# A delta-rule block: the state summed in PSUM, two tiles' joins interleaved, the experts' weights folded later, roots and pieces of the second inversion in another order

## The chip, the cores and the metric

One core of one Trainium2 chip. The time is microseconds (us) of device time for one launch, as the median of several runs; the profile is of one execution, recorded by the hardware profiler.

## The reference, cut to what matters

```python
# x: 4 sequences, 1024 tokens, 128 channels, float32
def delta(x, gates_w, gates_b, lr_w, lr_b, out_w, out_b):
    q, k, v = split(x @ gates_w + gates_b, 3)
    lr = x @ lr_w + lr_b
    k = k / norm(k)
    A = tril(k @ k.T, -1) + eye(T)          # T = 1024
    u = solve_triangular(A, v, lower=True)
    y = (q @ k.T) @ (lr * u)
    return y @ out_w + out_b
xn = layernorm(x)
h  = xn + delta(layernorm(xn), ...)
x1 = x + h + mlp(layernorm(h))              # 128 -> 128 -> 128, relu
z  = layernorm(x1)
chosen = argmax(z @ gate_w.T)               # 8 experts
out = x1 + z + z @ expert_w[chosen].T
```

The score matrix has no mask, so y = q @ M with M the sum over all tokens of k (lr u) as an outer product. The solve is done by tiles of 128 tokens with a running state S, the sum of k u over the tiles so far: u_t = T_t (v_t |k| - k_t S), where T_t is the inverse of the tile's lower triangle.

## The kernel before, in words

Everything is float32. T = 8 tiles of 128 tokens, each with NS = 4 sequences, so each tile is 128 x 512. Every engine has its program written out by hand in its own block (`@block.tensor`, `@block.vector`, `@block.scalar`, `@block.gpsimd`, `@block.sync`), in the order in which it is to run; semaphores are the only link. Nothing is planned or scheduled by a tool, so what a line waits for also holds up what stands behind it on its engine.

**Start (0 to 39 us).** VectorE takes the layernorm statistics (`stats`, `scales`, lines 688 to 714), ScalarE the square roots (`root`, L358), and the normalised tiles (`xh`) are written in pieces of one sequence by GpSimd, ScalarE and VectorE, as the tables XH_POOL, XH_ACT and XH_DVE say. TensorE turns a tile (`xT_`, L1048), multiplies by the weights of k (`kT_`, L1065), and takes the Gram matrix of the tile (`gram`, L1053); ScalarE evacuates each (`xnT_` L368, `kT_` L372, `gg_` L387). `k_` (L1048, evacuated by L376) turns k back for tiles 0 to 3 in the loop's second half. The sync engine copies the diagonal 32 x 32 blocks of the Gram matrices by DMA into `gd` (L264, 4 DMAs a tile).

**Inversions.** The 32 x 32 diagonal blocks of tiles 0 to 3 (group 0) are inverted together on VectorE, then those of tiles 4 to 7 (group 1): `prepare` (transpose L759, reciprocal L763, product L765), 31 steps of `eliminate` (L782 and L789), `plain_` and `place` (transposes L797 and L806, copies L811), `rest` (L816, L817). The steps of group 1 are cut into pieces between which VectorE does its share of the fold.

**Joins.** From the inverted 32-blocks TensorE builds the 128 x 128 inverse `tt_all` of each tile, with small matmuls and an evacuation after each: `ya` (L1124), `za` (L1133, L1136, L1141), `y64_` (L1150), `t12` (L1160). ScalarE's functions of the same names evacuate them; for tiles of group 1 VectorE takes `yb`, `zb` and `t12`. ScalarE's `diagonals` (L445, L448) and VectorE's `place` bring the inverted blocks to where the joins read them; PLACES says for which tiles at a time.

**Fold.** For each tile t, in the order of the loop at L1243: `ks` (k S, L1214), the rest of tile t's join, the next tile's `ya`, `w_` (u, L1220), `m_` of the tile before (L1232, summed in PSUM over all tiles), the next tile's `za`, `s_` (k u of this tile, L1224), and the next tile's `y64_`. VectorE's `rv_` (L839) makes the right side from the product ks. The state is in SBUF (`sm`): after each tile VectorE adds the four products that TensorE left in PSUM to it, one addition a sequence (`s_`, L844), and the next `ks` of a sequence waits for its addition; for tile 0 ScalarE copies them (L533).

**Experts' weights.** They are centred by matmuls of 512 columns (`expert_` L1110, `expert_one` L1114), two halves, placed between the joins and the folds of tiles 0 and 1; ScalarE evacuates them (L436).

**Tail (122 to 232 us).** M is multiplied out, and then for each tile: y (`delta`), second layernorm, MLP, choice of expert, 8 experts' products (L1324) and the pick of the chosen one on VectorE (L969).

```python
for t in range(T):            # TensorE, start
    kT_(t)
    if t + 1 < T: xT_(t + 1)
    gram(t)
    if t >= TG: k_(t - TG)
```

## Time and profile before

| | |
|---|---|
| median of the runs | 236.33 us (3 runs, 234.13 to 236.86) |
| the profiled execution | 233.88 us |
| its span, first to last instruction | 232.1 us |
| TensorE busy | 203.6 us (88%) |
| VectorE busy | 164.5 us (71%) |
| ScalarE busy | 122.8 us (53%) |
| GpSimd busy | 58.9 us (25%) |
| mean granted TensorE clock | 0.924 of full |

Some 1.8 us of the execution's time lie outside its span. The profile gives TensorE's granted clock per stretch: 1.00 is 2.4 GHz, 0.50 is 1.2 GHz, and values between are a mean of the two.

### The profile page before, as it was taken

To read this page: it belongs to the slowest core of one execution; us is meant where nothing else is said; L and a number is where in the kernel's file an instruction comes from. 1 tells how busy PE (TensorE), PEld (TensorE's weight loads), DVE (VectorE), ACT (ScalarE), POOL (GpSimd) and SP (SyncE) were. 2 spreads that over 40 slices of the span, in tenths; PEclk is the share of its full clock that TensorE was granted. 3 is DMA by queue.
4 is the path that set the end of the run, shared out by engine and by line. 5 is a ranking of instruction groups with operands and counts; after the bars stand their busy time and mean duration, and the time that the engine had idled before them with its cause. 6 is when DMAs were issued, how large, how long until landed. Compare 5 with 4: busy or idle time off the path is not lost.

```text
span 232.1 us, 4284 instructions
## 1 busy us (share of the span) xinstructions
PE 203.6 (88%) x1347; PEld 146.6 (63%) x1347; DVE 164.5 (71%) x748; ACT 122.8 (53%) x324; POOL 58.9 (25%) x73
## 2 busy tenths in 40 slices
PE   0795988999999759999989498999999999999980
PEld 0454666977799658989987285565656565565520
DVE  7994999999489854142353825969696878787785
ACT  2585565789585652434672555354646373735130
POOL 7255800000000069740200402206060606022020
PEclk9999799999999975557999859999999999999998
DMA  5951011000000000000000000001010101010111
GB/s 137 265 138 26 3 24 21 6 3 0 3 4 0 3 0 0 4 0 0 4 0 3 1 0 0 0 3 47 0 45 1 48 1 45 0 45 3 45 47 45
DMA packets 15612, 5.92 MB, mean 26 GB/s; under 512 B 5468, under 2 KB 15590, under 8 KB 15590
## 3 DMA queue, kind: packets, MB, share of 16 engines
q1 hardware_dynamic: 15014, 5.58, 9.6%
q8 instruction: 11, 0.18, 0.3%
q10 hardware_dynamic: 576, 0.07, 0.2%
q14 instruction: 11, 0.09, 0.1%
HBM read 3.09 MB, written 2.10 MB: 22 GB/s over the span
## 4 chain that ended last, share of the span: by engine, by line
PE 72%; DVE 8%; ACT 5%; issue 3%; DVEq 0%; ACTq 0%
PE ps L1324 22%; PE ps L1053 8%; PE ps L1048 5%; PE ps L1220 4%; PE ps L1224 4%; PE ps L1214 4%; PE ps L1232 3%; PE ps L1080 3%; PE ps L1299 3%; PE ps L1315 3%; PE ps L1150 2%; PE ps L1160 2%; DVE kT_all L969 2%; PE ps L1124 2%; ACT tt_all L448 1%
## 5 line engine op out<-in xcount | busy, mean ns | idle before, releaser
L1324 PE MATMUL ps<-ewC,kT_all 128*128 128x512 f32 x128 | 60.4, 596 | 0.9 <-DVE kT_all L969 0.8
L969 DVE COPY_PREDICATED kT_all<-mask,ps 128x256 f32<-128x256 int32 x112 | 48.9, 436 | 17.2 <-ACT kT_all L634 11.1
L1324 PEld LDWEIGHTS ps<-ewC,kT_all 128*128 128x128 f32 x128 | 22.0, 190 | 19.2 <-issue 19.2
L315 POOL TENSOR_SCALAR h_all<-x_all,mv,rr 128x128 f32<-128x128 f32 x16 | 12.4, 790 | 54.9 <-DVE da_all L817 54.9
L333 POOL TENSOR_TENSOR x_all<-x_all,kT_all 128x512 f32<-128x512 f32 x7 | 8.9, 1270 | 55.4 <-ACT kT_all L640 55.4
L789 DVE TENSOR_TENSOR xi<-xi,prod 128x60 f32<-128x60 f32 (+13 forms) x116 | 19.5, 207 | 0.3
L782 DVE TENSOR_TENSOR prod<-lts,xi 128x60 f32<-128x60 f32 (+13 forms) x116 | 19.3, 206 | 0.3
L328 POOL TENSOR_TENSOR x_all<-x_all,h_all 128x512 f32<-128x512 f32 (+1 forms) x9 | 10.3, 1147 | 30.9 <-DVE h_all L900 24.1
L611 ACT ACTIVATE k_all<-h_all,nb,rr 128x128 f32<-128x128 f32 x32 | 14.0, 484 | 4.2 <-DVE nb L921 4.2
L839 DVE SCALAR_TENSOR_TENSOR rv<-v_all,nk,ps 128x128 f32<-128x128 f32 x28 | 8.4, 345 | 10.0 <-PE ps L1214 9.5
L1048 PE MATMUL ps<-ident,h_all 128*128 128x128 f32 x32 | 6.0, 320 | 9.4 <-ACT h_all L363 7.0
L634 ACT COPY kT_all<-ps 128x256 f32<-128x256 f32 x16 | 5.8, 363 | 15.6 <-PE ps L1324 15.6
L1048 PEld LDWEIGHTS ps<-ident,h_all 128*128 128x128 f32 x32 | 4.7, 168 | 14.9 <-issue 14.6
L299 POOL TENSOR_SCALAR h_all<-x_all,mv,rr 128x128 f32<-128x128 f32 x14 | 11.1, 804 | 10.6 <-DVE rr L710 10.6
L322 POOL TENSOR_TENSOR x_all<-x_all,b2s 128x512 f32<-128x512 f32 x8 | 10.1, 1268 | 12.0 <-ACT h_all L527 12.0
L1220 PE MATMUL ps<-rv,tt_all 128*128 128x128 f32 x64 | 10.9, 323 | 1.4 <-DVE tt_all L832 0.6
L1053 PE MATMUL ps<-kT_all 128*128 128x128 f32 x64 | 9.9, 303 | 2.3 <-ACT kT_all L372 2.3
L1053 PEld LDWEIGHTS ps<-w2s,k_all 128*128 128x128 f32 x64 | 9.2, 208 | 4.0 <-issue 3.3
L1053 PEld LDWEIGHTS ps<-kT_all 128*128 128x128 f32 x64 | 8.4, 205 | 4.5 <-ACT kT_all L372 4.4
L1053 PEld LDWEIGHTS ps<-gg_all,xnT_all 128*128 128x128 f32 x64 | 9.1, 209 | 3.0 <-issue 2.4
L1220 PEld LDWEIGHTS ps<-rv,tt_all 128*128 128x128 f32 x64 | 9.4, 225 | 2.1 <-DVE rv L839 1.4
L1315 PEld LDWEIGHTS ps<-gwC,kT_all 128*128 128x128 f32 x64 | 8.5, 193 | 3.3 <-issue 3.3
(160 smaller groups left out, 437.4 us busy)
## 6 DMA issues: line engine op xcount, KB each, us to landing
x_all<-in_L_attn_x_dram SPq DMA_DIRECT2D x7, 256.0 KB, 5.5
out_dram<-x_all SPq DMA_DIRECT2D x7, 256.0 KB, 2.3
ew<-in_L_ffn_expert_w_dram SPq DMA_DIRECT2D x1, 512.0 KB
gd<-gg_all SPq DMA_DIRECT2D x28, 16.0 KB, 1.8
x_all<-in_L_attn_x_dram SPq DMA_DIRECT2D x2, 128.0 KB, 2.6
out_dram<-x_all SPq DMA_DIRECT2D x2, 128.0 KB, 1.8
wall<-in_L_attn_gates_w_dram SPq DMA_DIRECT2D x2, 64.0 KB
wall<-in_L_attn_gates_w_dram ACTq DMA_DIRECT2D x1, 64.0 KB, 2.6
```

What stands on the lines that cost most here:

```text
L299: nc.gpsimd.tensor_scalar(xh[:, t, n], x_all[:, t, n], mv[:, 0, t, n, 0:1], rr[:, t, 1, n:n + 1], ALU.subtract, ALU.mult).then_inc(xh_pool, 1)
L315: last = nc.gpsimd.tensor_scalar(h_all[:, t, n], x_all[:, t, n], mv[:, 0, t, n, 0:1], rr[:, t, 0, n:n + 1], ALU.subtract, ALU.mult)
L328: nc.gpsimd.tensor_tensor(x_all[:, t, span(of)], x_all[:, t, span(of)], h_all[:, t, span(of)], ALU.add).then_inc(xb_ready, len(of))
L611: nc.scalar.activation(tn[t % 2][:, n], h_all[:, t, n], ACT.Identity, bias=nb2[:, t, n:n + 1], scale=rr2[:, 0, t, n:n + 1]).then_inc(tn_re ...
L782: nc.vector.tensor_tensor(mul[half], lts[:, j, lo:hi].unsqueeze(2).broadcast_to([P, hi - lo, w]), xi[g][:, j, 0:w].unsqueeze(1).broadcast_ ...
L789: nc.vector.tensor_tensor(xi[g][:, lo:hi, 0:w], xi[g][:, lo:hi, 0:w], mul[half], ALU.subtract).then_inc(elim, 1)
L969: nc.vector.copy_predicated(sel[t % 2][:, n], mask[t % 2][:, n, E - 1 - e].unsqueeze(2).broadcast_to([P, 2, F]), ps[:, b:b + 2, (e % EH) * ...
L1048: last = nc.tensor.transpose(tiles(bank)[:, n], src(n), ident[:])
L1053: last = nc.tensor.matmul(tiles(bank)[:, n], lhsT(n), rhs(n), start=True, stop=True)
L1220: nc.tensor.matmul(ps[:, n, C:2 * C], tt_all[:, t, n], rv[:, n], start=True, stop=True).then_inc(w_mm, 1)
L1315: last = nc.tensor.matmul(ps[:, 3, n * E:n * E + E], x1T[t % 2][:, n], gwC[:], start=True, stop=True)
L1324: last = nc.tensor.matmul(ps[:, 4 + 2 * half + n, :], x1T[t % 2][:, 2 * pair + n], ewC[:, EH * half:EH * half + EH, :].rearrange("p e f -> ...
```

## The change

It has five parts.

1. **State in PSUM.** `s_` on TensorE no longer writes a product per tile that VectorE adds: it sums into bank 6 over all tiles (start on the first matmul of tile 0, no stop before tile 6), and signals once, after the fourth sequence. ScalarE copies the whole bank to `sm` (one 128 x 512 copy a tile); `ks` waits for that copy. VectorE's 24 additions (tiles 1 to 6) and ScalarE's 4 copies of tile 0 go. `yb` and `zb` move from bank 6 to bank 7.
2. **Joins.** `ya(1)` and `za(1)` stand before the first fold, `y64_(1)` ahead of the first `ks`, and on ScalarE rv0 is made early (so `norms`, the transpose of the norms, stands inside the first elimination). In the fold at t = 3, `ya(4)` stands between the two halves of `m_(2)`.
3. **Experts' weights.** `expert_` and `expert_one` move behind the fold, among the first `delta`s and transposes of the tail; the weights' halves use banks 4 and 5.
4. **Start.** `root(4)` and `root(5)` stand earlier on ScalarE, VectorE's statistics of tiles 6 and 7 stand behind the scaling of tiles 4 and 5, `xh` of tiles 4 to 7 has three pieces on GpSimd and one on VectorE (2 and 2 before), and `k_` stands ahead of `gram` (TensorE) and of `gg_` (ScalarE).
5. **Second inversion.** The pieces are cut at steps 9 and 22 (9, 19 and 27 before), both transposes stand ahead of `rv` of tile 3, the copies are made for tile 4 first and for tiles 5 to 7 behind; the product at L765 leaves out what the elimination does not read. The residual's `h_` of sequences 2 and 3 moves from ScalarE to VectorE.

```diff
-    XH_POOL = [()] + [LOW] * (T - 1)
+    XH_POOL = [()] + [LOW] * (TG - 1) + [(0, 1, 2)] * TG
-    XH_DVE = [HIGH] + [(3,)] * (TG - 1) + [HIGH] * TG
+    XH_DVE = [HIGH] + [(3,)] * (T - 1)
...
-        PLACES = ((0, 0, AHEAD), (0, AHEAD, TG), (1, 0, TG))
+        PLACES = ((0, 0, AHEAD), (0, AHEAD, TG), (1, 0, AHEAD), (1, AHEAD, TG))
...
@@ ScalarE, the start @@
             for t in range(T):
+                if t == TG - 2:
+                    root(4)
                 kT_(t)
+                if t == TG - 1:
+                    root(5)
                 if t + 1 < T:
                     xnT_(t + 1)
...
-                gg_(t)
-                if t == TG - 2:
-                    root(4)
                 if t >= TG:
                     k_(t - TG)
+                gg_(t)
+                if t == TG:
+                    nkl_(0)
...
@@ ScalarE, the fold @@
-            def s_(n):
-                act.wait_ge(s_mm, n + 1)
-                nc.scalar.copy(sm[:, n], ps[:, n, 2 * C:3 * C]).then_inc(s_ready, 1)
+            def s_(t):
+                act.wait_ge(s_mm, t + 1)
+                nc.scalar.copy(rows(sm[:, :, :]), ps[:, 6, :]).then_inc(s_ready, 1)
...
@@ VectorE, the start @@
+            stats(3)
             for j in range(2, len(PARTS)):
-                if j % 2 == 0:
-                    if j > 2:
-                        stats(j)
-                    stats(j + 1)
+                if j > 3:
+                    stats(j)
                 scales(j)
...
@@ VectorE, the product of prepare @@
-                nc.vector.tensor_tensor(lts[:], lt[:], rd[:].unsqueeze(1).broadcast_to([P, Q, Q]), ALU.mult).then_inc(elim, 1)
+                for lo, hi in ((0, 12), (12, Q - 1)):
+                    nc.vector.tensor_tensor(lts[:, lo:hi, lo + 1:Q], lt[:, lo:hi, lo + 1:Q],
...
@@ VectorE, the order @@
-            eliminate(1, 9, 19)
-            s_all(1)
+            eliminate(1, 9, 22)
             rv_all(2)
-            eliminate(1, 19, 27)
-            s_all(2)
+            eliminate(1, 22, Q - 1)
+            plain_(1)
+            turned(1)
             rv_all(3)
-            eliminate(1, 27, Q - 1)
-            plain_(1)
             place(2)
...
@@ TensorE @@
             def ks(t, n):
-                pe.wait_ge(s_ready, (t - 1) * NS + n + 1)
+                pe.wait_ge(s_ready, t)
...
             def s_(t, n):
                 pe.wait_ge(w_ready, t * NS + n + 1)
-                nc.tensor.matmul(ps[:, n, 2 * C:3 * C], k_all[:, t, n], ww[t % 2][:, n, 0:C], start=True,
-                                 stop=True).then_inc(s_mm, 1)
+                last = nc.tensor.matmul(tiles(6)[:, n], k_all[:, t, n], ww[t % 2][:, n, 0:C], start=t == 0 and n == 0,
+                                        stop=t == T - 2, skip_group_check=True)
+                if n == NS - 1:
+                    last.then_inc(s_mm, 1)
...
             delta(0, HIGH, 3)
+            expert_(0)
             delta(1)
+            expert_one(0)
             tT_(0, LOW)
+            expert_(1)
             hid_(0, LOW)
             tT_(0, HIGH, 6)
+            expert_one(1)
             out_(0, LOW)
```

On VectorE, the end of the second inversion. `xi` and `prod` are the elimination, `rv` the right side of the fold, `sm` the state; before, the last steps stand behind tile 2's addition and tile 3's right side:

```order
L844 TENSOR_TENSOR sm<-ps,sm 128x128 x4
L839 SCALAR_TENSOR_TENSOR rv<-v_all,nk,ps 128x128 x4
L782 TENSOR_TENSOR prod<-lts,xi 128x28 x2
L789 TENSOR_TENSOR xi<-xi,prod 128x2x14 x2
...
L789 TENSOR_TENSOR xi<-xi,prod 128x16
L797 STREAM_TRANSPOSE d_all<-xi 128x512
L806 STREAM_TRANSPOSE dT_all<-d_all 128x512
L811 COPY tt_all<-dT_all 32x16x32 x2
```

The same place of the changed kernel:

```order
L785 TENSOR_TENSOR xi<-xi,prod 128x16
L793 STREAM_TRANSPOSE d_all<-xi 128x512
L798 STREAM_TRANSPOSE dT_all<-d_all 128x512
L839 SCALAR_TENSOR_TENSOR rv<-v_all,nk,ps 128x128 x4
L808 COPY tt_all<-dT_all 32x4x32 x2
L817 COPY da_all<-d_all 32x16x32
L821 COPY yT<-ps 32x128
```

The right side of tile 3 now stands behind all of the elimination and both transposes, and no addition of the state is left.

On TensorE, from the first fold (L1220, then L1222) to the second tile's `ks` (L1214, then L1216). Before:

```order
L1220 MATMUL ps<-rv,tt_all 128x128 x4
L1224 MATMUL ps<-ww,k_all 128x128 x4
L1133 MATMUL ps<-yT,da_all 32x32 x4
L1136 MATMUL ps<-da_all,yT 32x32 x4
L1141 MATMUL ps<-yT,d_all 32x32 x4
L1110 MATMUL ps<-ewT,cent 128x512
L1214 MATMUL ps<-sm,kT_all 128x128 x4
```

Changed:

```order
L1136 MATMUL ps<-yT,da_all 32x32 x4
L1139 MATMUL ps<-da_all,yT 32x32 x4
L1144 MATMUL ps<-yT,d_all 32x32 x4
L1222 MATMUL ps<-rv,tt_all 128x128 x4
L1226 MATMUL ps<-ww,k_all 128x128 x4
L1153 MATMUL ps<-tt_all,gg_all 64x64 x4
L1216 MATMUL ps<-sm,kT_all 128x128 x4
```

`za(1)` went ahead of the first fold, the experts' matmul away, and `y64_(1)` in its place.

## Rows read from the trace of the kernel before

**Rows 1.** The page, second part: granted clock in 40 slices of 5.8 us.

```profile
PEclk9999799999999975557999859999999999999998
```

**Rows 2.** Windows: length; busy PE, PEld, DVE, ACT, POOL; granted clock; DMA share, GB/s.

```profile
18.70:22.50 3.80, 1.68 (x10) 0.88 (x9) 1.66 (x7) 1.39 (x3) 2.49 (x4) 1.00 0.17 26
...
78.40:84.00 5.60, 2.60 (x32) 2.29 (x32) 4.87 (x13) 4.47 (x12) 0.57 (x1) 1.00 0.01 3
84.00:107.80 23.80, 23.65 (x184) 21.61 (x186) 7.10 (x22) 8.05 (x27) 15.56 (x19) 0.50 0.00 1
...
126.00:131.70 5.70, 3.10 (x20) 2.15 (x18) 4.94 (x17) 1.97 (x6) 2.71 (x3) 1.00 0.01 1
131.70:138.60 6.90, 5.90 (x23) 4.83 (x23) 2.18 (x12) 4.22 (x11) 0.00 (x0) 0.51 0.00 0
```

**Rows 3.** Chain that ended last, fold: start us, us, what.

```profile
57.01 1.13 PE ps L1220 x8
...
61.00 0.89 PE ps L1214 x8
...
88.31 2.00 PE ps L1214 x8
...
99.98 2.00 PE ps L1214 x8
...
110.24 1.09 PE ps L1214 x8
...
117.12 1.09 PE ps L1214 x8
...
122.33 1.06 PE ps L1277 x4
```

**Rows 4.** Timeline of the start, all engines: start us, us, instruction, [idle before].

```profile
19.66 0.25 DVE L710 RECIPROCAL rr<-sd 128x16 f32<-128x16 f32 x1 [0.99 <-ACT sd L358]
...
20.01 3.16 POOL L299 TENSOR_SCALAR h_all<-x_all,mv,rr 128x128 f32<-128x128 f32 x4 [4.31 <-DVE rr L710]
...
25.65 1.97 DVE L759 STREAM_TRANSPOSE lt<-gd 128x1024 f32<-128x1024 f32 x1
```

**Rows 5.** Sync's last DMA of tiles 0 to 2, and its landing.

```profile
22.01 0.60 SPq L264 DMA_DIRECT2D gd<-gg_all  x1
...
DMA to landing us min/median/max: 1.8/1.8/2.9
```

**Rows 6.** The chain in the start's loop, one tile.

```profile
30.04 1.16 PE ps L1053 x8
31.20 0.44 PE ps L1048 x4
...
32.54 0.70 ACT kT_all L372
```

**Rows 7.** Timeline of VectorE: end of the first inversion, parts of the second.

```profile
45.14 1.07 DVE L797 STREAM_TRANSPOSE d_all<-xi 128x512 f32<-128x512 f32 x1
...
51.80 1.23 DVE L765 TENSOR_TENSOR lts<-lt,rd 128x1024 f32<-128x1024 f32 x1
...
69.75 1.12 DVE L839 SCALAR_TENSOR_TENSOR rv<-v_all,nk,ps 128x128 f32<-128x128 f32 x4 [0.73 <-PE ps L1214]
...
79.39 1.06 DVE L797 STREAM_TRANSPOSE d_all<-xi 128x512 f32<-128x512 f32 x1
```

**Rows 8.** Timeline, ScalarE before the first fold and the experts' copy.

```profile
50.29 0.41 ACT L445 COPY da_all<-d_all 32x128 f32<-32x128 f32 x1
...
59.23 0.59 ACT L436 COPY ewC<-ps 128x512 f32<-128x512 f32 x1
```

**Rows 9.** Timeline of TensorE at the start of the tail.

```profile
129.87 0.44 PE L1048 MATMUL ps<-ident,k_all 128*128 128x128 f32 x2 [1.78 <-ACT k_all L611]
131.12 0.67 PE L1299 MATMUL ps<-k_all,w1s 128*128 128x256 f32 x2 [0.81 <-ACT k_all L617]
132.59 0.69 PE L1048 MATMUL ps<-ident,k_all 128*128 128x128 f32 x2 [0.80 <-ACT k_all L611]
```

More of the change, by code:

```diff
@@ L197, in parts @@
             return [(half, lo, hi) for half, lo, hi in ((0, j + 1, j + 1 + top), (1, j + 1 + top, Q)) if hi > lo]
-        ELIM = 3 + sum(2 * len(parts(j)) for j in range(Q - 1))
+        ELIM = 4 + sum(2 * len(parts(j)) for j in range(Q - 1))
         AHEAD = 1
+        PREP_BANK = (4, 4, 4, 4, 4, 5)
         block = ctx.enter_context(nc.Block())
@@ L494, in _ @@
             k_(4)
+            for n in range(NS):
+                rv0(n)
             v_(2)
@@ L510, in _ @@
             za(0)
+            v_(6)
+            y64_(0)
             v_(7)
-            y64_(0)
-            for n in range(NS):
-                rv0(n)
+            ya(1)
+            yb(1)
             t12(0)
+            zb(1)
+            za(1)
             def w_(t, n):
@@ L568, in _ @@
                 if t == TG - 1:
-                    for n in range(NS):
-                        lrw(t, n)
                     diagonals(2)
                     ya(t + 1)
-                    za(t + 1)
-                else:
-                    za(t + 1)
-                    for n in range(NS):
-                        lrw(t, n)
+                za(t + 1)
+                s_(t)
                 y64_(t + 1)
-                for i in range(max(0, 2 * (t - TG) + 1), 2 * (t - TG) + 3):
-                    h_(i)
-            h_(T - 1)
+                for n in range(NS):
+                    lrw(t, n)
+                if t == TG - 1:
+                    diagonals(3)
             t = T - 1
@@ L773, in eliminate @@
             def eliminate(g, start, stop):
-                done = ELIM * g + 3 + sum(2 * len(parts(j)) for j in range(start))
+                done = ELIM * g + 4 + sum(2 * len(parts(j)) for j in range(start))
                 sub_at = [done, done]
@@ L848, in rv_all @@
                     rv_(t, n)
-            def s_all(t):
-                for n in range(NS):
-                    s_(t, n)
             prepare(0)
-            eliminate(0, 0, Q - 1)
+            eliminate(0, 0, 14)
+            norms(0)
+            eliminate(0, 14, Q - 1)
             plain_(0)
+            turned(0)
             place(0)
@@ L865, in _ @@
             rv_all(1)
-            eliminate(1, 9, 19)
-            s_all(1)
+            eliminate(1, 9, 22)
             rv_all(2)
-            eliminate(1, 19, 27)
-            s_all(2)
+            eliminate(1, 22, Q - 1)
+            plain_(1)
+            turned(1)
             rv_all(3)
-            eliminate(1, 27, Q - 1)
-            plain_(1)
             place(2)
             rest(1)
+            yb(TG)
+            norms(1)
+            zb(TG)
+            place(3)
             dve.wait_ge(nk_done, NG)
-            for t in range(TG - 1, T):
-                if t >= TG:
-                    rv_all(t)
-                    t12(t)
+            dve.wait_ge(xT_mm, T)
+            for t in range(TG, T):
+                rv_all(t)
+                t12(t)
                 if t + 1 < T:
@@ L1120, in ya @@
                 joined(pe, zb_ready, t)
-                for bank, lo, ready in ((5, 0, ya_mm), (6, 2 * Q, yb_mm)):
+                for bank, lo, ready in ((5, 0, ya_mm), (7, 2 * Q, yb_mm)):
                     hi = lo + Q
@@ L1241, in _ @@
                 s_(0, n)
-            za(1)
-            expert_(1)
+            y64_(1)
             for t in range(1, T):
@@ L1258, in _ @@
                 if t == 1:
-                    pe.wait_ge(prep_ready, 6)
-                for n in range(NS):
+                    pe.wait_ge(prep_ready, 4)
+                for n in LOW:
                     m_(t - 1, n)
@@ L1263, in _ @@
                     ya(t + 1)
+                for n in HIGH:
+                    m_(t - 1, n)
                 if joins:
```

99 lines of the change are left out of this document (44 added, 55 removed).

## The prediction

> **What bounds the kernel now.** I read the page first, for the clock, then the windows of its odd slices, then the chain that ended last, then the timelines of the engines that the chain names. The execution took 233.88 us for a span of 232.1, so 1.8 us lie outside; the median of the runs is 2.45 us above it. A difference of 2% (4.7 us) is about what a measurement of this kernel tells from none.
>
> The slices show TensorE's clock at the full 2.4 GHz except in three places: one in the start, a long one at 84 to 108 us, one early in the tail [rows 1]. In the windows, each low stretch follows one in which TensorE waited much: busy 1.68 of 3.80 us before the first (0.50, that is 1.2 GHz), 2.60 of 5.60 before the long one, 3.10 of 5.70 before the third [rows 2]. The long one is the dearest thing in this profile: TensorE is busy 23.65 of 23.80 us there, at 0.50. The chain shows what it costs: from one `ks` to the next it is 99.98 - 88.31 = 11.67 us at the low level and 117.12 - 110.24 = 6.88 us at the full one [rows 3], so 4.8 us a tile. The fold from 57 us on is bound by TensorE's own matmuls, except at one place: after the right side of tile 3, VectorE still has the end of the second inversion before it; its first transpose starts only at 79.39 [rows 7], and the joins of tile 4 wait for it: 3.0 of the 5.60 us from 78.4 to 84.0 are idle on TensorE. That wait costs twice, as idle time and as low clock behind it.
>
> **The start.** Tile 4's pieces wait for the root, which stands behind an evacuation: VectorE was idle 0.99 us for it, GpSimd 4.31 us, and its four pieces take 3.16 us, 0.79 each [rows 4]. Now the root is due when its input is there, some 2.7 us earlier (about 17.2 in place of 20.01 for GpSimd's start). GpSimd has three pieces a tile for four tiles: 3 x 0.79 = 2.4 us a tile, tile 4 ready at 19.6, tile 7 at 26.8. TensorE, idle for 2.1 us in the window at 18.7 to 22.5 [rows 2], gets its input at once. The root of tiles 6 and 7 is then bound by their statistics, so VectorE ends its pieces at 22.0, and the copies for the inversion at 22.5. In TensorE's loop a tile takes 1.16 + 0.44 + 0.87 + 0.70 and some gaps = 3.24 us along the chain [rows 6]; the 0.44 of `k_` moves under the 0.70 of ScalarE's copy, so 2.80. Bounds for the first part: nothing, to 3.8 us (the 2.1 idle and half of the 3.4 us at low clock). I take 3.0, since VectorE's order holds the copy of tile 3; with four times 0.44 the first `v_` comes 3.0 + 1.8 = 4.8 us earlier. GpSimd's 2.4 us a tile is inside 2.8, so it is just hidden; were its pieces 20% dearer, it would bound the loop.
>
> VectorE does not gain as much, because of a queue that the change leaves alone: the sync engine issues the 12 DMAs of tiles 0 to 2 one behind the other, the last at 22.01, landing 1.8 us later [rows 5], so the first inversion can start at 23.9 at the soonest, where it started at 25.65 [rows 4]. That is 1.75 us, not 3.1. The cut product (372 + 361 elements of 1024, by 1.23 us [rows 7]: 0.9 us in two) gives 0.3 us to each inversion, and the norms' transpose takes 0.2 of the first. An inversion took 45.14 - 25.65 = 19.5 us [rows 4, 7], so the blocks, with two transposes of 1.07, come at 45.5, 1.9 us earlier than now, and the second inversion starts some 2 us behind, at 47.5.
>
> **Up to the first fold.** ScalarE starts `diagonals` at 50.29 [rows 8]; it will do so at 45.5 (both the blocks and the copy of `v_(5)` are there then). Between there and the first `w_` (57.01 [rows 3]) ScalarE is the bound, and it keeps its work: rv0 leaves (1.2 us), `v_(6)` comes in (0.5). `w_` starts at 52.2, 4.8 us earlier. From there to `ks` of tile 1 it took 61.00 - 57.01 = 4.0 us [rows 3], with `za(1)` and the experts' 1.10 us in it; now w 1.1, s 0.9, then one copy of 0.6 (a 128 x 512 copy took 0.59 [rows 8]) beside `y64_(1)`, 2.7 us. `ks` of tile 1 at 54.95: 6.05 us earlier.
>
> **The fold.** VectorE loses the six times four additions, of about a microsecond a tile. A `ks` waited in its sequence for one addition; now all wait for a copy of 0.6 us after the last product, and `y64_` of 0.6 us stands in the gap. Bounds: 0 if hidden, 0.6 a tile if it is not (3.6 in all); I take 0.05 a tile. ScalarE has the copy, but `h_` went to VectorE, four pieces of 0.3 us in stages in which VectorE has 2 us of work: hidden.
>
> The second inversion has 19.2 us of its own work from 47.5 on, and two right sides of 1.12 us [rows 7] between: nothing else now, so it ends at 69.0, and the two transposes of 1.06 at 71.2. (The 31 steps are 15.4 of the 19.2, half a microsecond each: cut 9 is at 55.6, when tile 1's right side is due, cut 22 at 63.7, when tile 2's is.) TensorE asks for tile 3's right side at 70.3, so the wait is put here now: 1.2 us of idle in place of the 3.0. Then `w_` of tile 3 at 71.5 (78.4 before), the copies for tile 4 alone behind 1.12 us of right side [rows 7], and half of `m_(2)` under them. To `ks` of tile 4 it is 5.2 us at full clock (the same products as from `w_` to `ks` in a tile of 6.88 us): 76.7, where it was 88.31 [rows 3]. 11.6 us earlier.
>
> From there to the end of the fold the work is the same. Before: 117.12 - 88.31 = 28.8 us for three tiles, two of them at the low clock; now 3 x 6.93 = 20.8: 8.0 us more. Sum so far 19.6 us. From `ks` of tile 7 to the end of `m_`, 5.2 us [rows 3], nothing changes.
>
> **The clock.** Everything above hangs on it. The window of the long low stretch shows that the clock does not come back by TensorE's being busy (23.65 of 23.80 us [rows 2]), so a fall inside the fold is dear: 23.8 us at 4.8 us a tile of 11.67 is 9.8 us. The idle time of the changed kernel is 1.2 us before the inverted blocks (VectorE's and ScalarE's gain differ), about 1 us before `y64_(0)` and 1.2 us before `w_` of tile 3, each among small matmuls; so none as long as the 2.1 and 3.0 us in rows 2; but the experts' matmuls, which filled the joins, are gone.
>
> Here the Trainium skill says otherwise: in TensorE: Matmul & The Clock Gate, section "What's actually happening", "the default state is throttled, and activity releases the throttle". By that rule a fall in the fold would end soon and cost 1 or 2 us. The trace disagrees, with the 23.65 busy us at 0.50.
>
> **The tail.** TensorE was idle 1.78 + 0.81 + 0.80 us there, and then ran 6.90 us at 0.51 [rows 9, 2]. The experts' four matmuls (about 1.1 us each: 4.3 us) fill these gaps, and overflow them by 0.9. ScalarE's two copies of 0.59 [rows 8] delay the first transposes by 0.3 to 0.8. If the clock stays up, the 5.90 busy us at 0.51 become some 3: a gain of 2.1 net; if it falls all the same, a loss of 1.5. I take a gain of 1.5, since the gap before the low stretch is what is filled.
>
> **Sum.** 6.05 to `ks` of tile 1, 5.55 more to `ks` of tile 4, 8.0 in the tiles behind, 1.5 in the tail: 21.1 us. 233.88 - 21.1 = 212.8. The runs' median stood 2.45 above this execution; half of it, for low stretches that a run has more of, gives 214.0.
>
> **Rivals.**
> - *The clock falls in the fold* for a stretch like the one of before, now after the joins of tile 0 or before `w_` of tile 3. For it: three shorter waits stand where the clock held before, and nothing fills them. Against it: 1.2 us of idle is the most in one piece, and less than before each of the three falls. 214 + 9.8 = 223.8. With a quick release it is 216.
> - *The copy of the state and the new order are not hidden*: `ks` waits 0.6 us on six tiles, GpSimd's 12 pieces bound the start (1 us): 214 + 4.6 = 218.6. That the sum in PSUM saves nothing is this case too: the 24 additions lay beside TensorE's work but for the waits.
> - *Slower.* The clock falls at the joins of tile 0, where the experts' matmuls are gone, and does not come back before the tail, as it did not for 23.8 us of this fold's work [rows 2]. Then the seven tiles cost 4.8 us more each than in my sum: 214 + 33 = 247. It is slower than before from the fifth tile at low clock on. Against it: the same fold ran at full clock until 84.0 and again from 107.8 on [rows 1, 2].
>
> **How the numbers follow.** Forecast 0.58, a fall in the fold 0.25, the copy not hidden 0.12, the slow clock throughout 0.05. The first three are all faster by over 4.7 us. Faster 0.93, within 2% 0.03, slower 0.04. The time is the first case's, 214.0. Down, the start's and tail's bounds give 5 us (209); up, the range takes in the fall at 223.8: 209 to 225.
>
> **What would show it.** The inversion's first transpose at 24, the first `w_` near 52, `ks` of tile 4 near 77, no window at 0.50 between 70 and 100, the tile-to-tile step 6.9 throughout; 24 additions less on VectorE; an idle of about 1.2 us before tile 3's `w_`, put down to VectorE. I am wrong if the long low stretch is there again, elsewhere; if `ks` waits on ScalarE's copy by over 0.3 us a tile; or if the first inversion is not held by the DMAs.

## The result and the profile after

The changed kernel took 214.20 us (median of 4 runs, 213.98 to 214.80), the kernel before, on the same chip, 236.19 us (median of 4, 234.13 to 236.86): a ratio of 0.909, 95% interval 0.903 to 0.915. The profiled execution took 213.98 us for a span of 212.2. Span against span that is 19.9 us less, where the forecast's sum had 21.1. In 34 later executions the kernel before ran at one of two levels, 228.5 to 230.6 us with a mean granted clock of 0.949 to 0.959 (the lower) or 233.7 to 237.2 us with 0.923 to 0.925 (the upper), and the runs compared here lie at the upper one.

Two lines of the page, which answer to [rows 1]:

```profile
span 212.2 us, 4273 instructions
...
PEclk9999999999999999999999999999999999999998
```

The three places below 9 in [rows 1] are gone; the last slice is the end of the program. Windows of after, which answer to [rows 2]: the end of the second inversion, the four tiles behind it, and two stretches of the early tail. Columns: the stretch, its length, then busy time and instructions of PE, PEld, DVE, ACT and POOL, then the granted clock, the DMA share and GB/s.

```profile
69.00:75.00 6.00, 5.37 (x60) 4.72 (x59) 5.29 (x17) 4.78 (x16) 0.68 (x1) 1.00 0.00 0
75.00:99.00 24.00, 23.47 (x308) 20.98 (x306) 11.18 (x37) 14.14 (x47) 17.08 (x20) 1.00 0.01 3
112.00:118.00 6.00, 5.01 (x24) 2.75 (x23) 3.25 (x14) 4.68 (x12) 1.26 (x1) 1.00 0.00 0
118.00:124.00 6.00, 5.37 (x33) 3.83 (x32) 3.22 (x16) 3.08 (x9) 1.27 (x1) 1.00 0.00 0
```

TensorE is busy 5.37 of 6.00 us where it had 2.60 of 5.60, and 5.01 of 6.00 at the head of the tail where it had 3.10 of 5.70; behind each, the clock is 1.00 where it was 0.50 and 0.51. The chain that ended last, after, answers to [rows 3] (start, length, engine, tile and line; `L1216` is `ks`, `L1222` is `w_`, `L1279` the start of what follows the fold):

```profile
22.27 1.82 DMA gd<-gg_all
24.12 2.00 DVE lt L751
...
46.76 0.56 PE ps L1127 x16
...
53.08 0.88 PE ps L1222 x6
...
56.13 0.50 PE ps L1216 x2
...
72.41 1.24 PE ps L1222 x8
...
77.25 0.59 ACT sm L535
77.89 1.16 PE ps L1216 x8
...
84.91 1.16 PE ps L1216 x8
...
91.93 1.16 PE ps L1216 x8
...
98.95 1.16 PE ps L1216 x8
...
104.23 1.06 PE ps L1279 x4
```

Against before: `ks` of tile 1 comes 4.9 us earlier (61.00 to 56.13), `ks` of tile 4 10.4 us (88.31 to 77.89), `ks` of tile 7 18.2 us (117.12 to 98.95), and the rest, from 104.23 to the end of the span, is 108.0 us where it was 109.8. The step from `ks` to `ks` is 7.02 us from tile 4 to 5, 5 to 6 and 6 to 7, where it was 11.67, 10.26 and 6.88.

### The profile page after: what moved, and what is told of

It is laid out like the page before. It is cut to its first block, busy times and chain, and to the rows that moved or that the text cites. A ratio compares the mean times of both kernels' runs of the same rounds, so it can differ in the third digit from the quotient of the medians.

```text
span 212.2 us, 4273 instructions
## 1 busy us (share of the span) xinstructions
PE 190.4 (90%) x1347; PEld 135.0 (64%) x1347; DVE 161.2 (76%) x740; ACT 119.0 (56%) x314; POOL 62.4 (29%) x77
## 4 chain that ended last, share of the span: by engine, by line
PE 58%; DVE 24%; SPq 9%; issue 4%; ACT 3%; DMA 1%; DVEq 0%; ACTq 0%
PE ps L1326 24%; DVE xi L785 6%; DVE prod L778 6%; PE ps L1057 6%; PE ps L1052 4%; SPq L267 3%; PE ps L1222 3%; PE ps L1317 3%; PE ps L1301 3%; PE ps L1226 3%; PE ps L1236 3%; SPq L249 3%; PE ps L1216 2%; DVE kT_all L973 2%; SPq L259 2%
## 5 line engine op out<-in xcount | busy, mean ns | idle before, releaser
L318 POOL TENSOR_SCALAR h_all<-x_all,mv,rr 128x128 f32<-128x128 f32 x16 | 12.8, 816 | 45.5 <-DVE da_all L817 45.5
L302 POOL TENSOR_SCALAR h_all<-x_all,mv,rr 128x128 f32<-128x128 f32 x18 | 14.2, 806 | 7.6 <-DVE rr L703 7.6
L1057 PEld LDWEIGHTS ps<-w2s,k_all 128*128 128x128 f32 x64 | 8.5, 191 | 4.1 <-issue 3.8
L839 DVE SCALAR_TENSOR_TENSOR rv<-v_all,nk,ps 128x128 f32<-128x128 f32 x28 | 7.8, 338 | 4.3 <-PE ps L1216 4.3
L1222 PE MATMUL ps<-rv,tt_all 128*128 128x128 f32 x64 | 9.2, 286 | 1.5 <-DVE tt_all L832 0.6
L1057 PEld LDWEIGHTS ps<-gg_all,xnT_all 128*128 128x128 f32 x64 | 8.3, 191 | 3.3 <-issue 2.6
L608 ACT ACTIVATE k_all<-ps,cols 128x512 f32<-128x512 f32 (+1 forms) x9 | 6.6, 731 | 5.9 <-PE ps L1052 5.9
```

The costliest lines, as they stand in the source:

```text
L302: nc.gpsimd.tensor_scalar(xh[:, t, n], x_all[:, t, n], mv[:, 0, t, n, 0:1], rr[:, t, 1, n:n + 1], ALU.subtract, ALU.mult).then_inc(xh_pool, 1)
L318: last = nc.gpsimd.tensor_scalar(h_all[:, t, n], x_all[:, t, n], mv[:, 0, t, n, 0:1], rr[:, t, 0, n:n + 1], ALU.subtract, ALU.mult)
L1057: last = nc.tensor.matmul(tiles(bank)[:, n], lhsT(n), rhs(n), start=True, stop=True)
L1222: nc.tensor.matmul(ps[:, n, C:2 * C], tt_all[:, t, n], rv[:, n], start=True, stop=True).then_inc(w_mm, 1)
```

## The experiments

The runs stand in four series, each on another chip and each with runs of the kernel before in it: experiments 1 to 3, 4 to 7, 8 to 10, and 11. A kernel is compared with before at one of the two levels and with the changed kernel's 214.2 us; the changed kernel itself ran again in the second series alone (experiment 7). The lower level of before had medians of 228.7, 228.8, 229.1 and 229.0 us in the four, so a difference of under half a microsecond between series says little. For such differences two intervals of the trace are steadier, `ks` of tile 1 to `ks` of tile 4 and `ks` of tile 4 to `ks` of tile 7: in two traces of the changed kernel they are 21.76 and 21.06, and 21.77 and 21.06 us.

**1. Only the long wait filled.** The kernel before, with ten matmuls of 128 columns, whose result is not used, in TensorE's wait for the second inversion.

```diff
                 if t + 1 == TG:
+                    for i in range(7):
+                        nc.tensor.matmul(ps[:, 7, 0:C], ident[:], ident[:], start=True, stop=True)
                     ya(t + 1)
+                    for i in range(3):
+                        nc.tensor.matmul(ps[:, 7, 0:C], ident[:], ident[:], start=True, stop=True)
```

> The kernel before, with ten matmuls of 128 columns added on TensorE (into a corner of PSUM that nobody reads), seven before the joins of tile 4 and three behind their first step: work in place of the wait for the second inversion, nothing else changed. If the clock falls because TensorE waits there, the stretch at 0.50 from 84 to 108 us goes and with it 8 to 10 us: 226 to 228 us against 236. Rival: the low stretch comes from the fold's own work or from the chip, whatever TensorE does in the wait: then it stays, and the time is the same or 0.5 us longer.

Measured: 224.91 us (224.66 to 226.02, 4 runs), the lower level of before in the same series being 228.45 to 228.74 and the upper 236.84 to 237.16; ratio to the lower level 0.985 (0.981 to 0.988). The row of the granted clock, and the window where before had 23.65 busy us at 0.50 [rows 2]:

```profile
PEclk9999699999999999999999589999999999999998
```

```profile
84.00:108.00 24.00, 23.58 (x310) 21.36 (x309) 10.80 (x40) 15.24 (x50) 17.38 (x20) 1.00 0.01 2
```

What is left of TensorE's idle time there, 0.59 and 0.17 us where the kernel before had 2.12 and 1.03:

```profile
83.23 0.59 PE L1124 MATMUL ps<-tt_all,gg_all 32*32 32x32 f32 x16 [0.59 <-DVE tt_all L811]
...
84.85 0.31 PE L1133 MATMUL ps<-yT,da_all 32*32 32x32 f32 x5 [0.17 <-ACT yT L453]
```

Nothing of the kernel's own work was removed, and the kernel's own matmuls came no earlier to these places (83.23 where it was 82.53). So the low stretch comes from TensorE's being idle ahead of it. Filling the wait is worth 3.8 us against the lower level of before and 12 us against the upper, and the time is below the 226 to 228 us expected. The stretches in the start and in the tail stay. This is the claim under the whole forecast, shown with one edit.

**2. How thin is the margin?** The changed kernel, with one or three more transposes of some 1.1 us on VectorE (into a buffer that is no longer read) ahead of tile 3's right side. The edit with one; the other has `range(3)`.

```diff
             turned(1)
+            for i in range(1):
+                dve.wait_ge(dT_done, 2 + i)
+                nc.vector.transpose(xi[0][:].rearrange("p r k -> p (r k)"), xi[1][:].rearrange("p r k -> p k r")).then_inc(dT_done, 1)
             rv_all(3)
```

> As the one with three transposes, with one: TensorE waits 1.6 us. It shows how near the changed kernel stands to a fall. If it has room: 215.3 us and full clock. Rival: the fall is near, and some or all of the runs have a low stretch: 220 to 225 us.

> The changed kernel, with three more transposes of 1.1 us on VectorE (into a buffer that is free by then) ahead of the right side of tile 3, so that TensorE waits about 3.8 us there in place of 0.6. If the wait alone brings the clock down: 3.3 us for the transposes and up to 10 for a stretch at 0.50 behind it, 221 to 228 us against 214. Rival: the clock does not depend on this wait: 217.5 us and no window at 0.50.

Measured: one transpose 219.23 us (215.96, 220.13, 220.02, 218.44), three 221.74 us (220.03, 223.45, 219.10, 223.91). The granted clock goes with the time: 0.998, 0.967, 0.967, 0.972 and 0.982, 0.960, 0.989, 0.961. TensorE's timeline at tile 3's `w_` in the first and the second kernel, the idle time ahead and its releaser in brackets:

```profile
74.33 1.26 PE L1225 MATMUL ps<-rv,tt_all 128*128 128x128 f32 x8 [1.61 <-DVE rv L839]
```

```profile
76.96 1.97 PE L1225 MATMUL ps<-rv,tt_all 128*128 128x128 f32 x8 [3.75 <-DVE rv L839]
```

The profiled runs are the fastest of the four with one transpose (215.96) and the second fastest with three (220.03). The wait grew from 0.56 to 1.61 and 3.75 us. With 1.61 the clock held in the profiled run, and `ks` of tile 1 to `ks` of tile 4 took 22.84 us, 1.08 more than in the changed kernel: the length of the transpose. The rest of that run's 1.8 us lay ahead of the edit, in the start, where the changed kernel's own two traces differ by 0.7 us (experiment 7). In the other three runs the mean clock was 0.967 to 0.972 and the cost 4.2 to 5.9 us; they have no trace, so that their low stretch lies behind this wait is argued, not shown. Behind the wait of 3.75 eight `w_` matmuls took 1.97 us in place of 1.26. The price of a wait here is its length plus, in some runs, a low stretch.

**3. The order of the second inversion undone**, its cuts at 19 and 27 and its end behind tile 3's right side, with VectorE's copies for tiles 4 to 7 together, as before; the rest of the change stays, ScalarE's order, the shorter product and `h_` on VectorE among it.

```diff
-            eliminate(1, 9, 22)
+            eliminate(1, 9, 19)
             rv_all(2)
-            eliminate(1, 22, Q - 1)
+            eliminate(1, 19, 27)
+            rv_all(3)
+            eliminate(1, 27, Q - 1)
             plain_(1)
             turned(1)
-            rv_all(3)
             place(2)
+            place(3)
+            norms(1)
             rest(1)
             yb(TG)
-            norms(1)
             zb(TG)
-            place(3)
```

> The changed kernel with the order of the second inversion as before: cuts at 9, 19 and 27, right side of tile 3 ahead of the last steps and the transposes, and the copies for tiles 4 to 7 in one piece. By my steps the end of the inversion moves from ahead of tile 3's right side to behind it: tile 3's fold comes 2 us earlier, but the joins of tile 4 wait some 3 us for the last steps, the transposes and the copies; structurally 1 to 2 us slower, 216, and 224 to 226 if that wait brings the clock down. Rival: the order of the pieces is worth nothing by itself, since the additions that went have freed VectorE: 214 to 214.5.

Measured: 221.32 us (221.15 to 222.43, 4 runs), 7.1 us above the changed kernel, with clocks of 0.968 to 0.976. That lies between the 216 us expected without a fall of the clock and the 224 to 226 with one. Its timeline of TensorE and its windows (columns as above):

```profile
76.90 0.87 PE L1128 MATMUL ps<-tt_all,gg_all 32*32 32x32 f32 x16 [2.15 <-DVE tt_all L808]
82.97 2.07 PE L1217 MATMUL ps<-sm,kT_all 128*128 128x128 f32 x8
93.23 1.16 PE L1217 MATMUL ps<-sm,kT_all 128*128 128x128 f32 x8
```

```profile
70.90:76.90 6.00, 3.29 (x28) 2.87 (x28) 5.21 (x21) 3.34 (x12) 0.00 (x0) 0.99 0.00 0
76.90:85.50 8.60, 8.60 (x73) 7.68 (x74) 3.42 (x10) 4.21 (x13) 6.94 (x9) 0.50 0.01 2
```

The wait of 2.15 us is that of before, and it brings the low stretch back: `ks` of tile 4 is 5.1 us later than in the changed kernel, and one step is 10.26 us. Of the four pieces that were undone or added alone (experiments 3 to 6), this order is the largest.

**4. The start alone**, on the kernel before: the third piece of tiles 4 to 7 on GpSimd, the roots moved up, `k_` ahead of the Gram copy, and VectorE's statistics in the changed kernel's order (the last two are not shown).

```diff
-    XH_POOL = [()] + [LOW] * (T - 1)
+    XH_POOL = [()] + [LOW] * (TG - 1) + [(0, 1, 2)] * TG
...
-    XH_DVE = [HIGH] + [(3,)] * (TG - 1) + [HIGH] * TG
+    XH_DVE = [HIGH] + [(3,)] * (T - 1)
...
+                if t == TG - 2:
+                    root(4)
                 kT_(t)
+                if t == TG - 1:
+                    root(5)
...
```

> The kernel before with the start part alone (GpSimd's third piece for tiles 4 to 7, the roots of the second group before their turn, k_ ahead of the Gram copy). Theory (the start moves the joins earlier, and the later stages are bound by VectorE's two inversions and by the clock): the first v_ some 4 us earlier than 39.33 and the first inversion's transpose near 24, but ks of tile 1 only some 1.8 us earlier than 61.00, because the diagonals wait for the first inversion; then the second inversion, which keeps its order, is waited for as before (3 us idle before tile 4's ya), and the long stretch at 0.50 stays. Time 1.5 to 3 us below the kernel before at the same level: about 234 against 236.5, or 226.5 against 228.6. Rival (the start is worth its full 4 us down to the end): 224 to 225 against 228.6.

Measured: 225.24 us (224.52 to 225.46, 4 runs), all at clocks of 0.951 to 0.959; before at that level, same series, 228.46 to 228.86. That is 3.6 us below its median of 228.8, about the rival's number (224 to 225). The chain:

```profile
22.29 1.82 DMA gd<-gg_all
24.13 1.99 DVE lt L758
...
46.88 0.56 PE ps L1123 x16
...
57.27 0.89 PE ps L1213 x8
...
84.59 2.00 PE ps L1213 x8
```

`ks` of tile 1 and of tile 4 are both 3.7 us earlier than in [rows 3]. My theory had the first inversion hold the joins; but before, it was done by about 47.3 (45.14 us in [rows 7], plus two transposes of 1.07), and `diagonals` started only at 50.29 [rows 8], behind the `v_` copies. The inversion had 3 us to spare, so the start's gain went through: in this run `diagonals` starts at 46.40, behind a `v_` copy again. The wait for the second inversion stayed at 2.12 us and the low stretch behind it too, as the theory had it, but with one step of `ks` slowed in place of two.

**5. The experts' weights back among the joins** and in the fold's first tiles, with ScalarE's two copies of them.

```diff
             ya(0)
             v_(6)
+            expert_(0)
             za(0)
             v_(7)
             y64_(0)
+            expert_one(0)
             ya(1)
...
-            expert_(0)
             delta(1)
-            expert_one(0)
             tT_(0, LOW)
-            expert_(1)
...
```

> The changed kernel with the experts' four matmuls back among the joins and the fold's first tile, the two copies of ScalarE too. Theory (they fill gaps of the tail, which starves TensorE's clock without them): ks of tile 1 some 1 to 1.5 us later than 56.13 (ScalarE's 1.2 us of copies stand before the w_ copies), the tail from the end of m_ to the end 109.8 us as before in place of 108.0, with the stretch at 0.50 near 128 us back: 216 to 218. Rival (the tail's gaps are ScalarE's anyway and the clock holds): 214.5 to 215.5, PEclk at 9 to the end.

Measured: 218.79 us (217.65 to 219.84, 4 runs), clocks 0.979 to 0.981. Row of the clock, `ks` of tile 1 in the chain, and two rows of TensorE's timeline in the tail:

```profile
PEclk9999999999999999999996799999999999999997
```

```profile
58.39 0.89 PE ps L1219 x8
```

```profile
114.51 0.65 PE L1052 MATMUL ps<-ident,k_all 128*128 128x128 f32 x2 [1.78 <-ACT k_all L604]
115.97 1.19 PE L1307 MATMUL ps<-k_all,w1s 128*128 128x256 f32 x2 [0.81 <-ACT k_all L610]
```

The gaps of 1.78 and 0.81 us in [rows 9] are back, and so is the low stretch, now at about 113 to 124 us. The move is worth 4.6 us on the medians, more than the 2 to 4 expected. In the profiled run, the fastest of the four, it is 2.3 at `ks` of tile 1, which I had priced at 1 to 1.5, another 0.5 by `ks` of tile 4, and 0.9 behind the fold. That run's first inversion also started 0.5 us earlier (23.64), so the joins lost 2.8 us rather than 2.3.

**6. The state added up on VectorE again**, from a product in each tile's own bank, where the changed kernel sums in PSUM.

```diff
+            def sadd(t):
+                for n in range(NS):
+                    dve.wait_ge(s_mm, t * NS + n + 1)
+                    nc.vector.tensor_tensor(sm[:, n], ps[:, n, 2 * C:3 * C], sm[:, n], ALU.add).then_inc(s_ready, 1)
...
-            eliminate(1, 9, 22)
+            eliminate(1, 9, 20)
+            sadd(1)
             rv_all(2)
-            eliminate(1, 22, Q - 1)
+            eliminate(1, 20, 29)
+            sadd(2)
+            eliminate(1, 29, Q - 1)
```

> The changed kernel with the state added up on VectorE out of SBUF again, 24 additions of some 0.26 us, in the new order of the second inversion. Theory (their price is the delay of the second inversion): two groups of four stand before the inversion's end, so tile 3's right side comes 2 us later than 72.0 and ks of tile 4 some 2 us later than 77.9; 216 to 217 if the clock holds, 219 to 224 if the wait of 2.5 us before tile 3's w_ lets it fall, as in the run with three transposes more. Rival (the additions lay beside TensorE's work, as before): 214 to 214.8, ks of tile 4 within 0.5 us of 77.9.

Measured: 216.27 us as a median, but in two pairs: 214.80 and 214.91 us at clocks of 0.996 and 0.997, 217.64 and 218.17 at 0.980 and 0.981. The rows of the profiled run (one of the pair at the higher clock), `ks` of tile 2, tile 3's `w_`, and `ks` of tiles 4 and 5:

```profile
63.88 1.16 PE L1225 MATMUL ps<-sm,kT_all 128*128 128x128 f32 x8 [1.03 <-DVE sm L850]
...
73.83 1.26 PE L1231 MATMUL ps<-rv,tt_all 128*128 128x128 f32 x8 [1.34 <-DVE rv L838]
79.19 1.16 PE L1225 MATMUL ps<-sm,kT_all 128*128 128x128 f32 x8
86.07 1.16 PE L1225 MATMUL ps<-sm,kT_all 128*128 128x128 f32 x8
```

The additions make `ks` of tile 2 wait 1.03 us, since here they stand behind eleven steps of the inversion, and delay tile 3's `w_` by 1.4 us; a part is won back, since a tile then takes 6.88 us again. The span is 213.1, 0.9 above the changed kernel's. So at the full clock the sum in PSUM is worth 0.7 us. In two runs of four the mean clock was lower, and there it is worth 3.7; which of the two waits, 1.03 or 1.34 us, that goes with isn't shown, since these runs have no trace. The cuts differ too (9, 20 and 29), so other places for the additions could cost less.

**7. The changed kernel once more**, unedited.

> The changed kernel itself, once more, on this chip, to see whether it has two levels as the kernel before has (228.6 and 236.9). Theory (its waits are too short for the clock to fall): 213.9 to 214.9 in every run, granted clock 0.99 to 1.0. Rival (the thin margin that the runs with one and three transposes more showed is crossed by itself on some runs): one or more runs of 217 to 221, clock below 0.98.

Measured: 214.19 us (214.81, 213.93, 214.09, 214.29), clocks 0.993 to 1.0. In eight runs it has one level, where the kernel before has two. The profiled run (214.81) is 0.8 us slower than the first profiled one, and nearly all of that is in the start: the first inversion's transpose at 24.76 in place of 24.12, `ks` of tile 1 at 56.83 in place of 56.13, and 21.77 us from there to `ks` of tile 4.

**8. The copy of the state in two halves**, each `ks` waiting for its own.

```diff
-                nc.scalar.copy(rows(sm[:, :, :]), ps[:, 6, :]).then_inc(s_ready, 1)
+                for of in (LOW, HIGH):
+                    nc.scalar.copy(sm[:, span(of)], tiles(6)[:, span(of)]).then_inc(s_ready, 1)
...
-                pe.wait_ge(s_ready, t)
+                pe.wait_ge(s_ready, 2 * t - 1 + n // 2)
```

> The changed kernel with ScalarE's copy of the summed state in two halves, each ks waiting for its half alone. Theory (the one copy of 0.59 us that four ks wait for is the 0.14 us by which a tile takes 7.02 in place of 6.88): the step from ks to ks falls to 6.88 and the span by 0.8 to 1.0 us, to 211.3; time 213.3. Rival (two copies cost ScalarE more than they free, some 0.2 us a tile in fixed cost, and push the y64_ copy and the left sides): step 7.0 to 7.1, time 214.2 to 215.

Measured: 213.19, 213.53 and 213.78 us at clocks of 0.994 to 1.0, and 216.06 at 0.947; median 213.66. The profiled run is the one at 0.947. In its chain, `ks` of the last four tiles:

```profile
77.99 1.10 PE ps L1217 x8
...
84.89 1.09 PE ps L1217 x8
...
91.78 1.09 PE ps L1217 x8
...
98.68 1.09 PE ps L1217 x8
```

A step of 6.90 in place of 7.02: the term that the forecast had at 0.05 a tile was 0.14, and the halves give 0.12 of it back. From `w_` of tile 0 to `ks` of tile 7 the fold takes 45.31 us in place of 45.94; six steps would give 0.7, but tile 3's `w_` now waits 0.78 us for its right side. The three runs at the higher clock, 213.5 in the middle, are 0.7 below the changed kernel's 214.2, which ran in another series; experiment 10 has the step at 6.88 in a run at 0.998.

**9. The cuts of the second inversion moved to where VectorE has no wait**, 10 and 25 in place of 9 and 22.

```diff
-            eliminate(1, 0, 9)
+            eliminate(1, 0, 10)
...
-            eliminate(1, 9, 22)
+            eliminate(1, 10, 25)
             rv_all(2)
-            eliminate(1, 22, Q - 1)
+            eliminate(1, 25, Q - 1)
```

> The changed kernel with the cuts of the second inversion placed where VectorE has no wait: the right side of tile 1 after 10 steps in place of 9, that of tile 2 after 25 in place of 22. Theory (VectorE waits 0.84 and 1.26 us for TensorE before these two right sides, and this wait is what makes tile 3's right side late): the second inversion's transposes come 1.5 to 2 us earlier (69.98 to some 68.2), tile 3's w_ no longer waits for them (0.56 us of TensorE's idle goes), ks of tile 4 at 77.2 to 77.4 in place of 77.89, time 213.5 to 213.8. Rival (what the steps gain, ks of tiles 1 and 2 lose by a right side that now comes late): ks of tile 4 at 77.8 or later, time 214.2 to 215.

Measured: 215.15 us (214.94 to 215.46, 4 runs), 1 us slower than the changed kernel and slightly above the rival's range. From `ks` of tile 1 to `ks` of tile 4 it took 22.46 us in place of 21.76, so 0.7 of it is the cuts' own. I had read the changed kernel's waits in sum and put one of 1.26 us to tile 2's right side. Its timeline shows that this piece had no wait at all (rows of VectorE, changed kernel):

```profile
56.77 1.12 DVE L839 SCALAR_TENSOR_TENSOR rv<-v_all,nk,ps 128x128 f32<-128x128 f32 x4 [0.84 <-PE ps L1216]
64.76 1.11 DVE L839 SCALAR_TENSOR_TENSOR rv<-v_all,nk,ps 128x128 f32<-128x128 f32 x4
```

The 1.26 us stood before tile 4's right side. With the cut at 25 tile 2's came at 66.00, and TensorE waited for it (same kernel, TensorE):

```profile
66.39 1.26 PE L1222 MATMUL ps<-rv,tt_all 128*128 128x128 f32 x8 [0.72 <-DVE rv L839]
73.50 1.13 PE L1222 MATMUL ps<-rv,tt_all 128*128 128x128 f32 x8 [0.56 <-ACT tt_all L483]
```

**10. The edits of 8 and 9 together, and the eight DMAs of the later weights issued behind the Gram matrix's 12** of the first inversion.

```diff
-            for dst, src in ((wo[:, :], out_w), (w1s[:, :], w1), (w2s[:, :], w2), (bor[:, :], out_b.unsqueeze(0)),
...
             for t in range(T):
                 if t == TG - 1:
+                    for dst, src in ((wo[:, :], out_w), (w1s[:, :], w1), (w2s[:, :], w2), (bor[:, :], out_b.unsqueeze(0)),
...
                     continue
```

> Both edits together, and the eight DMAs of the weights issued behind the Gram matrix's 12 of the first inversion in place of ahead of them. Theory (the three add up, each for its own wait): the first inversion's transpose 0.3 to 0.4 us earlier than 24.12, the step 6.88, span 212.2 - 0.35 - 0.9 - 0.55 = 210.4, time 212.2. Rival (they do not add: TensorE's own work bounds the joins, and the DMAs moved back delay the second group's): 213.3 to 214.2.

Measured: 214.11 us (213.47 to 214.49, 4 runs), where 212.2 was expected: the rival. The step is 6.88, and the cut at 25 takes back what it gives: tile 2's `w_` waits 0.86 us for its right side. The first inversion's transpose starts at 23.97, which is within what it differs by in runs with no edit ahead of it (23.64 in experiment 5, 24.76 in experiment 7), so a gain from the DMAs' place isn't shown.

**11. The same with the cut at 23.**

> As cuts_half_weights, with tile 2's right side after step 23 in place of 25 (tile 1's after 10). Theory (with 25 it came at 66.00 where TensorE asked at 65.4, and that cost the 1 us that the three edits together did not give): tile 2's w_ has no wait, the second inversion still ends half a microsecond earlier than in the changed kernel, and the three edits add up: ks of tile 4 at 77.1 to 77.4, span 210.9 to 211.2, time 212.8 to 213.1. Rival (tile 4's joins are bound by ScalarE's left sides as in the last two runs, whatever VectorE does): ks of tile 4 at 77.6 or later, time 213.4 to 214.

Measured: 213.37 us (median of 6: 212.65, 212.71, 213.01, 213.72, 213.73, and 217.76 at a clock of 0.974); ratio to the lower level of before 0.930 (0.926 to 0.934). TensorE's timeline, `w_` of tiles 2 and 3 and `ks` of tile 4:

```profile
64.87 1.13 PE L1222 MATMUL ps<-rv,tt_all 128*128 128x128 f32 x8
...
71.71 1.13 PE L1222 MATMUL ps<-rv,tt_all 128*128 128x128 f32 x8 [0.56 <-DVE rv L839]
76.94 1.16 PE L1216 MATMUL ps<-sm,kT_all 128*128 128x128 f32 x8
```

Tile 2 has no wait, tile 3's `w_` still waits 0.56 us for its right side, and the span is 210.9. `ks` of tile 4 is 0.95 us earlier than in the changed kernel: 0.42 of it was there at `ks` of tile 1, and 0.53 comes between the two (21.23 us in place of 21.76). Behind it three steps of 6.88 give 0.42 more. Five of six runs are below the lowest of the changed kernel's eight (213.93), with a median of 213.01, 1.2 us below its 214.2; with the sixth run it is 0.8. The changed kernel did not run in this series, and with one run of 217.76 I would not say that this one is steadier.

## Why the prediction was right, and where it was off

The forecast was 214.0 us (209 to 225), faster with 0.93; 214.20 was measured, and 214.19 again. The mechanism came as forecast: the three low stretches went, and experiment 1 shows for the long one that the wait was its cause. The total is nearer than its terms.

- *The start.* Forecast: the inversion's transpose at 23.9, held by the DMAs; measured 24.12, with the landing of the DMAs ahead of it in the chain. The start's loop took 2.80 us a tile, as forecast, and the first `v_` came at 35.03 (4.3 us earlier, not 4.8). GpSimd's twelve pieces were hidden.
- *Up to the first fold.* This is the step that was too large: `ks` of tile 1 was to be 6.05 us earlier and was 4.9. `diagonals` started at 46.09 on ScalarE where I had 45.5; the cut product took 1.18 and 0.99 us where I had 0.9. From there to the first `w_` I named a net gain of 0.7 us (1.2 out, 0.5 in) and took none, with 6.7 us; it was 7.0. From the first `w_` to `ks` it was 3.05 us, not 2.75. The copy of 0.59 us stood in the forecast; what was too small were the products, since the copy waits for the last of them: `w_` to `s_` took 1.22 us where I had 1.1, `s_` to the copy 1.20 where I had 0.9. Of the 4.9, the start alone gives 3.7 (experiment 4).
- *The fold up to tile 4.* 5.55 us more were forecast, and 5.5 came (10.4 less 4.9). Tile 3's `w_` was forecast at 71.5 with 1.2 us of idle, and stood at 72.41 with 0.56. VectorE came 0.9 us late to this place: the second inversion began at 47.89 where I had 47.5, and inside it tile 1's right side waited 0.84 us for the late `ks`, where I had it run without a wait. From `w_` of tile 3 to `ks` of tile 4 it was 5.5 us, not 5.2. Undone, this order costs 7.1 us (experiment 3).
- *The last tiles.* Forecast 8.0 us with steps of 6.93; measured 7.8, with steps of 7.02. The difference is the copy, at 0.14 us a tile where I had 0.05 (experiment 8).
- *The tail.* Forecast 1.5, measured 1.8, with the low stretch gone. Put back, the experts' matmuls cost 4.6 us in all (experiment 5), more than their tail alone: I had not counted what they cost in the joins.
- *The offset.* I added 1.2 us since the runs of before lay 2.45 above their profiled one, and put that down to low stretches. The changed kernel's median lies 0.2 above its own profiled run. The reason was not borne out either: at its upper level before ran 233.7 to 234.5 us in three runs and 236.1 to 237.2 in fifteen, all at a mean clock of 0.923 to 0.925, so the clock does not tell them apart. The sum was 1.2 us too large and the offset 1.0 too large. They cancelled, and the hit to 0.2 us is luck to that extent.

*The rivals.* That the clock falls in the fold did not come in any of eight runs, but it was near: with an operation of 1.1 us more, three runs of four were at a mean clock of 0.967 to 0.972 (experiment 2). The rival with the copy not hidden was right in kind and at a quarter of its size (0.14 us a tile in place of 0.6). The clock low through the whole fold did not come in any kernel here.

Of the rule that I weighed, in the Trainium skill, TensorE: Matmul & The Clock Gate, section "What's actually happening", that activity releases the throttle: the runs again show stretches that TensorE's activity did not end at once (8.60 busy of 8.60 us at 0.50 in experiment 3), and with the same work they were of different length (one step of `ks` was slowed in experiment 4, from 84.59 to 94.80 us, and two in the profiled run of before). That the clock falls when TensorE waits agrees with the page; experiment 1 shows it with one edit.

*The account.* Against the lower level of before, 228.7 us, the change is worth 14.5 us. Four parts were measured by one edit each: the start 3.6, the order of the second inversion 7.1, the experts' move 4.6, the sum in PSUM 0.7, together 16.0. They overlap, and the start was measured on the kernel before, the others on the changed one, so this is no exact sum. The interleaving of the joins (part 2 of the change) was not undone alone, nor were the shorter product and the move of `h_`: what they are worth isn't shown. The 22.0 us of the first comparison contain some 7.5 us more, by which before is slower at its upper level.

*What stays open.* Why the same program of before has a long and a shorter low stretch in different runs. With experiment 4's start alone all four runs were at the lower level, and whether the edit did that or chance isn't known. Why the runs at the upper level differ by 2 to 3 us at the same mean clock. And why one run of the last kernel, with shorter waits than the changed kernel's, had a clock of 0.974. No profile was taken of before at its lower level, nor of that run.

## What to carry to other kernels

Look at the clock row first, and behind each low stretch for the wait on TensorE ahead of it: here waits of 2.1 and 1.0 us among small matmuls cost 4 to 12 us, and filling them with useless matmuls gave that back, which is a cheap test before anything is reordered. Work that can stand anywhere (the experts' weights) belongs where TensorE starves, and an engine's long serial work (the inversion) should give way to another's request only where that request is due, which is read from the timeline, not from the sum of waits. The distance of a median from its profiled run is not to be carried over to a changed kernel: here it was 2.45 us before and 0.2 after. An edit worth less than a microsecond is read from an interval of the trace between two of the kernel's own events, since the start alone differed by 0.7 us between two runs of one kernel.

## What the runs showed of the hardware that was not expected

- The mean granted clock of one program takes separate values in different runs: 0.949 to 0.959 in sixteen runs of before and 0.923 to 0.925 in eighteen, and nothing between. That this is the length of the long stretch is read from traces of two kernels (two slowed steps of `ks` in the profiled run of before, at 0.924; one in experiment 4, at 0.951), not from two runs of one.
- One run of experiment 8 had a mean clock of 0.947 with no low stretch: it was 1.00 from 5 to 8 us, and 0.94 or 0.95 in every window read from 15 us on. The four windows of a quarter of a microsecond from 142 to 143 us read 0.95 each, so in this run a value between 0.50 and 1.00 is not the mean of stretches at the two levels, as far as such windows tell.

```profile
40.00:104.00 64.00, 60.71 (x752) 55.06 (x751) 47.27 (x228) 43.99 (x146) 17.81 (x20) 0.95 0.01 2
...
130.00:160.00 30.00, 30.00 (x131) 17.94 (x130) 22.67 (x96) 15.85 (x39) 7.55 (x6) 0.95 0.06 18
```

In that run a matmul of 128x512 took 616 ns between 130 and 190 us, and 594 ns in the changed kernel:

```profile
L1327 PE MATMUL ps<-ewC,kT_all 128*128 128x512 f32 x84 | 41.3, 616 | 0.0
```

```profile
L1326 PE MATMUL ps<-ewC,kT_all 128*128 128x512 f32 x88 | 41.5, 594 | 0.0
```

The clock row of the profile's page reads 9 throughout, as for a full clock; only the mean and the windows show it. That run's 216.06 us against 213.5 for the other three is its price. The fold paid nothing of it: the step of `ks` was 6.90 us there. From `ks` of tile 7 to the end of the span it was 115.6 us, where the changed kernel's took 113.3.

- A short low stretch also came at the joins of tile 0, in the run with three more transposes and ahead of the place of that edit: `w_` of tile 0 took 2.04 us, where the changed kernel's took 1.16, six microseconds behind a wait of 1.43 us. The changed kernel waits 1.33 us at that place and kept its clock in the profile.

```profile
46.89 0.56 PE L1130 MATMUL ps<-tt_all,gg_all 32*32 32x32 f32 x16 [1.43 <-DVE tt_all L808]
...
53.13 2.04 PE L1225 MATMUL ps<-rv,tt_all 128*128 128x128 f32 x8
```
